# Cross-attention block: the transposes of the probabilities on VectorE instead of TensorE, the product with the values in sixteen array tiles, the row sums on ScalarE

## The reference, cut to what matters

```python
# layer 0
q = x @ Wq.T + bq;  k = y @ Wk.T + bk;  v = y @ Wv.T + bv
x1 = softmax(where(mask == 0, NEG, q @ k.T)) @ v + x
# layer 1, per head of 32 channels
scores = (Q @ K.T) / sqrt(32)              # 2048 x 77 per batch and head
attn = softmax(scores, axis=-1)
context = attn @ V                         # 2048 x 32
out = layernorm(context @ W_o.T + b_o + x1) * gamma + beta
```

## Time and profile before

| | |
|---|---|
| median of 3 runs | 410.09 us (408.79 to 412.2) |
| the profiled execution | 408.65 us, its span 406.8 us |
| PE busy | 390.2 us, 96% of the span |
| DVE, ACT, POOL busy | 292.8, 260.7, 221.4 us (72%, 64%, 54%) |
| TensorE's granted clock | at the full level in nearly all slices (mean 0.996) |

### The profile page before, as it was taken

How to read it: one execution, slowest core, us unless ns; L and a number is a source line. 1 busy time by engine, 2 the same in 40 slices (tenths; PEclk the granted TensorE clock), 3 DMA queues, 4 the chain that set the end, 5 groups by cost and what they waited for, 6 DMA issues and landing times.

```text
span 406.8 us, 12216 instructions
## 1 busy us (share of the span) xinstructions
PE 390.2 (96%) x4984; PEld 298.0 (73%) x4984; DVE 292.8 (72%) x711; ACT 260.7 (64%) x780; POOL 221.4 (54%) x244
## 2 busy tenths in 40 slices
PE   8999998899999999999999999999999999999894
PEld 8869856577777877777777777677777777777663
DVE  0456477548867898678967986778867986657787
ACT  2333678765678674867578567857588558766820
POOL 0420377225547755776567754765478654763541
PEclk9999999999999999999999999999999999999998
DMA  8885003400032301421041303240042200251022
GB/s 301 305 312 210 12 3 118 136 3 3 2 129 86 131 2 28 171 95 56 2 162 54 131 2 122 93 131 2 3 161 97 88 2 16 81 174 61 2 105 103
DMA packets 17302, 37.56 MB, mean 92 GB/s; under 512 B 1808, under 2 KB 3344, under 8 KB 16223
## 3 DMA queue, kind: packets, MB, share of 16 engines
q1 hardware_dynamic: 16815, 36.24, 26.0%
q10 hardware_dynamic: 432, 0.54, 0.4%
HBM read 26.49 MB, written 8.39 MB: 86 GB/s over the span
## 4 chain that ended last, share of the span: by engine, by line
PE 83%; ACT 11%; DVE 2%; DMA 2%; issue 1%; SPq 0%; DVEq 0%
PE ps_q L958 22%; PE ps_out L1023 20%; PE ps_t L983 14%; PE ps_s L972 7%; PE ps_pv L998 6%; PE ps_out L918 5%; ACT prob L503 3%; ACT pt L512 3%; ACT y L524 2%; PE ps_s L884 2%; PE ps_s L1041 2%; ACT q L467 1%; PE ps_s L897 1%; DMA raw<-in_w0k 1%; PE ps_t L1086 1%
## 5 line engine op out<-in xcount | busy, mean ns | idle before, releaser
L360 POOL TENSOR_TENSOR prob<-prob,rc 128x308 f32<-128x308 f32 x128 | 91.2, 719 | 126.0 <-DVE rc L712 125.8
L503 ACT ACTIVATE prob<-ps_s,mx 128x77 f32<-128x77 f32 x512 | 121.9, 324 | 1.8 <-DVE mx L703 1.8
L512 ACT ACTIVATE pt<-ps_t 77x512 f32<-77x512 f32 x128 | 76.2, 595 | 61.4 <-PE ps_t L983 60.9
L710 DVE TENSOR_REDUCE sm<-prob 128x4 f32<-128x308 f32 x128 | 59.5, 465 | 37.0 <-ACT prob L503 36.8
L983 PE MATMUL ps_t<-ident,prob 128*77 128x128 f32 x512 | 79.2, 277 | 3.1 <-ACT pt L512 3.1
L983 PEld LDWEIGHTS ps_t<-ident,prob 128*77 128x77 f32 x512 | 61.6, 147 | 21.5 <-issue 7.6
L703 DVE TENSOR_REDUCE mx<-ps_s 128x4 f32<-128x308 f32 x128 | 53.9, 469 | 23.1 <-PE ps_s L972 23.1
L335 POOL TENSOR_TENSOR x_l<-x_raw,x_h 128x512 fp32r<-128x512 f32 x32 | 44.6, 1398 | 21.9 <-ACT x_h L449 11.7
L958 PE MATMUL ps_q<-x_h,wq_h 128*128 128x512 f32 x128 | 53.2, 415 | 0.0
L958 PE MATMUL ps_q<-x_h,wq_l 128*128 128x512 f32 x128 | 53.0, 414 | 0.0
L972 PEld LDWEIGHTS ps_s<-k1T,q 32*64 32x64 f32 x2048 | 25.8, 130 | 27.8 <-issue 15.0
(11 more groups left out here) (130 smaller groups left out, 605.4 us busy)
## 6 DMA issues: line engine op xcount, KB each, us to landing
x_raw<-in_xT SPq DMA_DIRECT2D x8, 1024.0 KB, 7.4
y<-in_x SPq DMA_DIRECT2D x28, 256.0 KB, 2.7
out<-y SPq DMA_DIRECT2D x28, 256.0 KB, 2.0
mask_sb<-in_mask SPq DMA_DIRECT2D x8, 154.0 KB, 7.3
raw<-in_w0q SPq DMA_DIRECT2D x4, 256.0 KB, 5.9
raw<-in_w0v SPq DMA_DIRECT2D x1, 1024.0 KB, 10.1
raw<-in_w1q SPq DMA_DIRECT2D x1, 1024.0 KB, 12.7
raw<-in_w1k SPq DMA_DIRECT2D x1, 1024.0 KB, 5.0
```

The lines of the kernel that those rows point to most:

```text
L360: nc.gpsimd.tensor_tensor(ap, ap, wide(rc[:, k % 2, h], KEYS), ALU.mult).then_inc(prob_done, 1)
L503: e = nc.scalar.activation(prob[:, k % 2, h, t], ps_s[:, h, t * KEYS:(t + 1) * KEYS], ACT.Exp, bias=mx[:, k % 2, h, t:t + 1])
L512: nc.scalar.activation(pt[:, h], ps_t[0:KEYS, :], ACT.Copy).then_inc(pt_ready, 1)
L710: nc.vector.reduce_sum(sm[:, k % 2, h], prob[:, k % 2, h], AX_X).then_inc(sum_done, 1)
```

## The change

It touches layer 1 in four places, and the order of the work around them.

1. **Transposes.** PE no longer transposes the probabilities, and ACT no longer copies them out of PSUM. DVE transposes 32 by 32 blocks from SBUF to SBUF. The rows of `prob` are padded from 77 to 96 elements (the padding is zeroed once by POOL), and one DVE instruction handles a pair of heads, two for each unit. Such an instruction transposes only inside 32 by 32 blocks, so the keys of query rows 0 to 31 of a tile end in partitions 0 to 31, those of rows 32 to 63 in partitions 32 to 63, and so on.
2. **Context.** The product now runs as 3 parts of the keys x 4 quadrants of rows x 4 heads = 48 matmuls of 32 (the last part 13) x 32 weights and 128 moving columns, where it was 4 matmuls of 77 x 32 weights and 512 columns. The four quadrants write four PSUM banks (`ps_mid`, the last 128 columns of each); two of the four also hold scores. The values must stand in all quadrants, for which SP spreads them once, with seven DMAs at the start.
3. **Row sums.** DVE's sum is gone. Each exponential on ACT also gives its row sum (`accum_out`).
4. **Moves.** `round_x` goes from DVE to ACT, and parts of layer 0's softmax go on DVE from step g = 1 to step g = 0.

New waits: `context` waits for all exponentials of the following unit (`exp_done`), since it writes banks that they read. `round_ct` waits for the scores of the unit two further on (`s_done`), for the same reason.

```diff
-        pt = sb("pt", [KEYS, KC, BLOCK])
-        prob = sb("prob", [P, 2, GROUP_HEADS, TILES, KEYS])
+        pt = sb("pt", [P, GROUP_HEADS, PARTS, TILES, Q])
+        prob = sb("prob", [P, 2, TILES, GROUP_HEADS, PADDED])
...
@@ sync
+            sp.wait_ge(v1_ready, BATCH)
+            spread(0, 1, Q, KEYS - Q)
...
+            spread(3 * Q, 2, 2 * Q, LEFT)
@@ scalar
                 wait(act, max_done, heads(i, k, h) + 1)
+                wait(act, t_done, pairs(i, k - 2, h // 2) + 1)
                 for t in range(TILES):
-                    e = nc.scalar.activation(prob[:, k % 2, h, t], ps_s[:, h, t * KEYS:(t + 1) * KEYS], ACT.Exp, bias=mx[:, k % 2, h, t:t + 1])
+                    e = nc.scalar.activation(prob[:, k % 2, t, h, 0:KEYS], ps_s[h][:, t * KEYS:(t + 1) * KEYS], ACT.Exp,
+                                             bias=mx[:, k % 2, h, t:t + 1], accum_out=sm[:, k % 2, h, t:t + 1])
...
-                nc.scalar.activation(pt[:, h], ps_t[0:KEYS, :], ACT.Copy).then_inc(pt_ready, 1)
...
                 wait(act, pv_done, units(i, k) + 1)
-                nc.scalar.activation(ct_h[:, k // CH % 2, k % CH], ps_pv[:], ACT.Copy).then_inc(cth_ready, 1)
+                if k + 2 < UNITS:
+                    wait(act, s_done, units(i, k + 2) + 1)
+                nc.scalar.activation(rows_in_quadrants(ct_h[:, k // CH % 2, k % CH]),
+                                     ps_mid[:, :, PV:512].rearrange("p i (t r) -> p i t r", r=Q), ACT.Copy).then_inc(cth_ready, 1)
@@ vector
+            def transposes(i, k, a):
...
+                own = slice(2 * a, 2 * a + 2)
+                wait(dve, prob_done, heads(i, k, 2 * a + 1) + 1)
+                wait(dve, pv_done, units(i, k))
+                nc.vector.transpose(pt[:, own].rearrange("p h n t r -> p t (h n) r"),
+                                    prob[:, k % 2, :, own].rearrange("p t h (n r) -> p t (h n) r", r=Q)).then_inc(t_done, 1)
...
-                nc.vector.reduce_sum(sm[:, k % 2, h], prob[:, k % 2, h], AX_X).then_inc(sum_done, 1)
-                wait(dve, sum_done, heads(i, k, h) + 1)
                 nc.vector.reciprocal(rc[:, k % 2, h], sm[:, k % 2, h]).then_inc(rcp_done, 1)
@@ tensor
-                    mm = nc.tensor.transpose(ps_t[0:KEYS, t * P:(t + 1) * P], prob[:, k % 2, h, t], ident[:])
...
-                wait(pe, pt_ready, heads(i, k, GROUP_HEADS))
+                wait(pe, t_done, pairs(i, k, PAIRS))
+                if k + 1 < UNITS:
+                    wait(pe, exp_done, heads(i, k + 1, GROUP_HEADS))
+                    to = [ps_mid[:, r, PV:512] for r in range(P // Q)]
...
-                    mm = nc.tensor.matmul(ps_pv[rows_of, :], v1[:, b % 2, own], pt[:, h], start=True, stop=True)
+                for n in range(PARTS):
+                    depth = Q if n + 1 < PARTS else LEFT
+                    for r in range(P // Q):
+                        keys = slice(r * Q, r * Q + depth)
+                        for h in range(GROUP_HEADS):
+                            own = slice(g * P + h * HEAD_DIM, g * P + (h + 1) * HEAD_DIM)
+                            mm = nc.tensor.matmul(to[r][h * HEAD_DIM:(h + 1) * HEAD_DIM, :], v1[keys, b % 2, slot(r, n), own],
+                                                  pt[keys, h, n].rearrange("p t r -> p (t r)"),
+                                                  start=(n == 0), stop=(n == PARTS - 1))
...
             def last_step():
-                transposes(0, UNITS - 1, 0)
-                last_output(0, 0, 2)
-                last_output(1, 0, 2)
...
                 last_output(2, 0, 2)
                 last_output(3, 0, 2)
...
+                for t in range(TILES):
+                    last_output(t, 2, 8)
+                last_output(0, 8, 11)
                 context(0, UNITS - 1)
...
+                for t in range(1, TILES):
+                    last_output(t, 8, 11)
+                for t in range(TILES):
+                    last_output(t, 11, OUTPUT)
```

219 lines of the change are left out of this document (123 added, 96 removed).

## The result

The changed kernel takes 423.57 us (median of 4 runs, 422.39 to 426.15); the kernel before took 409.58 in the same comparison. The ratio is 1.033, with a 95% interval of 1.0295 to 1.0365: it is slower, where 388.5 us and faster were forecast. The profiled run has a span of 421.8 us and a mean granted clock of 0.945 (before: 406.8 us, 0.996).

A forecast was written before the change was run, and what follows sets the result against it. PE, busy 96% of the span, was taken as the bound. Six blocks -22.8, three later steps -3.6, start +0.5 and tail +4.3 gave -21.6 us: median 388.5 us, with 375 to 416 for 8 in 10.

The forecast's parts named there:

- a: On ACT: price of a row sum beside each exponential, sixteen times a step, taken as 0.10 us, between 0.04 and 0.144.
- rival 2: On ACT: the row sum is dear at 0.206 us and ACT becomes the bound, 425 us, slower than before; chance 0.17.
- rival 3: In context on PE: sixteen tiles don't work side by side, 3.0 us in place of 1.5, 436 us; chance 0.08.
- A transpose on DVE: On DVE: 768 elements take 0.96 us, eight a block 7.7 us; from above, half the rate, 1.9 us.
- rival 4: On DVE: its transposes run at half rate, 7.6 us more in a block, 407 us, no measurable change; chance 0.07.
- The longer of the two decides: In each step of a block, the longer of ACT's and PE's times counts: 40.55 us a block against 44.35.
- the 8.3 and the 10.6: Steps g = 0 and g = 3: lengths in us set by ACT's chain of exponentials and the new waits.
- A sign that did not come: On PE: idle ahead of context in g = 0 and g = 3, not g = 1 and 2, released by ACT's exponentials.
- The half clock: On PE: the forecast is wrong if its clock falls below full level in the new waits; no size given.
- Start and tail: Outside the six blocks: the start was to cost +0.5 us and the tail +4.3 us.
- the first of the last statistics: In the tail: the last block's first statistics come 21.1 us after the last scores, where they came 16.8 us after.
- 79% of a block: On DVE: its busy share of a 40.55 us block, up from 72%, as sums gone and transposes added about cancel.

The follow-up runs named there:

- e18: Changed kernel with long matmuls between context's key parts, two scores matmuls doubled in g = 1, the g = 3 waits taken out, x loaded early: 410.75 us, ratio 1.001.
- e16: Changed kernel with layer 0's transposes behind four query matmuls, rest of context behind two maxima, first normalise behind the last exponentials, all in g = 3: 416.91 us.
- e12: Changed kernel with 16 useless matmuls of 512 columns inside the 4.1 us wait for the exponentials in step k = 2: 424.59 us, ratio 1.038.
- e8: Changed kernel with later loads of x and mask cut to 16 partitions, 8 KB of x and some 20 KB of mask: 416.68 us, ratio 1.018.

## Why the prediction was wrong, point by point

**What was right.** The exponentials with a row sum start 0.30 us apart in place of 0.208:

```profile
197.35 0.32 ACT L535 ACTIVATE prob<-ps_lo,mx 128x77 f32<-128x77 f32 x1
197.56 0.20 ACT L535 ACTIVATION_READ_ACCUMULATOR prob<-ps_lo,mx 128x1 f32 x1
197.65 0.33 ACT L535 ACTIVATE prob<-ps_lo,mx 128x77 f32<-128x77 f32 x1
197.86 0.21 ACT L535 ACTIVATION_READ_ACCUMULATOR prob<-ps_lo,mx 128x1 f32 x1
```

So a = 0.092 us, forecast 0.10, and rival 2 (0.206, 425 us) has nearly the right time by the wrong mechanism. Context takes 1.42 to 1.49 us for 96 records, forecast 1.47, which also does away with rival 3. A transpose on DVE takes 0.95 us, forecast 0.96 (rival 4 out):

```profile
L760 DVE STREAM_TRANSPOSE pt<-prob 128x768 f32<-128x768 f32 x64 | 58.5, 950 | 0.0
```

**The step that failed.** "The longer of the two decides: 8.3 (ACT), 11.2 (PE), 10.45 (PE), 10.6 (ACT), in sum 40.55". A third bound was missing: the supply of PE's instructions. The prediction priced 48 matmuls by their time and gave their number no price. From scores(4) to scores(28) the kernel took 269.5 us, 44.9 a block. Of that 14.7 us are gaps and 10.2 half clock (added up from windows of half a microsecond); without them it is 244.6, or 40.8 a block, against 40.55. By the steps: g = 0 took 11.1 to 13.3 us for 8.3; k = 12 took 12.43, less 2.21 and 1.7 is 8.5. g = 1 took 10.8 (11.2 forecast), g = 2 10.5 to 11.9 (10.45). Against the kernel before the start took 4.7 us more, the six blocks 2.2 more, the three steps behind them 0.4 more and the tail 7.7 more, 15.0 in sum; forecast were +0.5, -22.8, -3.6 and +4.3.

**A sign that did not come.** PE was to stand idle ahead of context in g = 0 and g = 3, released by ACT's exponentials. In the six blocks the trace shows no such wait (7.7 us, all in k = 1, 2 and 31). In g = 0 PE had by then lost time of its own to the gap and the half clock behind it; in g = 3 it had waited 0.91 us ahead of the transposes of layer 0. So the changed kernel never shows the bound by ACT that the 8.3 and the 10.6 rest on, and that 40.8 comes so near to 40.55 is in part luck. e18, with few gaps left, does show a wait of PE for the exponentials, 1.04 us ahead of the context of each g = 3 from k = 7 to 27, but there context also comes ahead of the last two matmuls of the query.

**The half clock** was the last sentence of the prediction, "if PE's clock falls below the full level in the new waits, which no row before shows". It fell, in one wait at the start, one in the tail, and most often behind the gaps. I had it as a case with no chance of its own, yet the prediction itself let PE stand idle in g = 0 and g = 3.

**A wait that I missed.** In g = 3 the transposes of layer 0 wait 0.91 us for the low part of context, since the rounding now waits for `s_done`. I had put that delay on ACT's chain alone (10.6 us); the step took 10.85, near it but by PE, which is luck. The wait is 7.2 us in all, and e16, which takes it out with two smaller edits, gains 6.7.

**Start and tail.** scores(4) came 4.7 us later for 0.5. The wait of 4.1 us in k = 2 and the half clock behind it (5.1 us) stand there; e12 shows that the clock is not an extra cost there, since `p_b` is waited for anyway. The tail is 7.7 us longer for 4.3, of which 3.4 are the half clock behind the wait in k = 31; the first of the last statistics comes 24.6 us after the last scores, forecast 21.1.

**A slip that cost nothing.** DVE was to be busy for 79% of a block, since its sums and its transposes cancel. They do (59.5 us before, 58.5 now), but the rounding of x, which the prediction names as gone, was left in the sum: DVE's busy time fell from 292.8 to 261.8 us.

**What I could have read.** The chain of the kernel before has 1% issue. Its view of waits has it in layer 0, 128 short records in a row:

```profile
PE ps_out L918 <- issue: 1.8, 2, 1.0
```

Two gaps of 0.75 and 1.05 us, in layer 0, which in the steps of that kernel is the only stretch with over 100 short records in a row. Most of these stretches have no gap, so the view shows the risk and not its price. The change put such a stretch into every step.

**What stays open.** Why a fetch in steps with g = 3 waits for context, up to 5.5 us after the border, where most others start within 1.7 us of theirs. It is not the load of x alone: in e8, too, the fetch starts up to 4.7 us after the border and 0.5 to 0.9 us after context. Context is where PE's program waits for other engines, but no run takes these waits away one by one. Nor do I know why the gap of 2.05 us in k = 16 of the changed kernel is not followed by half clock.

## What to carry to other kernels

Count instructions, not only time: in this kernel a stretch in which PE uses 256 instructions in less than about 3.5 us risks a gap if a border falls into it. That is an estimate, from 2.4 us between the start of a fetch and its use and about 1 between the border and that start; in g = 3 the second part was up to 5.5 us. Look for "issue" on the busiest engine before replacing few long matmuls by many short ones, put long ones between them, and keep large loads away from that place. And a stop of PE may be paid twice, the second time by half clock: behind the 16.5 us of gaps here stand 11.9 us of lost clock. The other 11.3 us of that column stand behind the two long waits for the exponentials (5.1 and 3.4) and at the very end (2.8, where the kernel before has its 1.6 too).
